# The third layer of an MLP on one Trainium2 core: its inputs as the fixed operand, the weight column moving, one answer a partition

## What is computed

```python
h = jnp.concatenate([z, dense_ctx], axis=1)      # 2048 x 208
h = jnp.maximum(h @ W_top1 + b_top1, 0.0)        # 208 -> 512
h = jnp.maximum(h @ W_top2 + b_top2, 0.0)        # 512 -> 256
y = h @ W_top3                                   # 256 -> 1, no bias
```

## Time and profile before

| what | value |
|---|---|
| median of three runs | 1182.02 us (1181.14 to 1182.32) |
| the profiled execution, its time | 1184.45 us |
| its span, first to last instruction | 1182.6 us |
| TensorE clock granted, mean | 0.99 of full speed |
| PE / PE weight load busy | 1118.4 us (95%) / 395.6 us (33%) |
| DVE / ACT / POOL busy | 1111.5 us (94%) / 835.7 us (71%) / 917.6 us (78%) |
| DMA packets, bytes | 76480, 167.32 MB |

### The profile page before, as it was taken

The page is one execution under the profiler, slowest core; times in us unless marked ns, Lnnn a source line. Parts: engine busy times, 40 slices in busy tenths (PEclk is TensorE's granted clock), DMA queues, the critical chain, the costliest instruction groups (busy, mean ns, idle before and its releaser), DMA issues.

```text
span 1182.6 us, 15683 instructions
## 1 busy us (share of the span) xinstructions
PE 1118.4 (95%) x5312; PEld 395.6 (33%) x5312; DVE 1111.5 (94%) x509; ACT 835.7 (71%) x2385; POOL 917.6 (78%) x640
## 2 busy tenths in 40 slices
PE   0587999999999999999999999999999999999997
PEld 0122233333333333333333333333333333333343
DVE  0598999999999999999999999999999999999994
ACT  0466577677868777686877778687767868777782
POOL 6767888888888888888888888888888888884400
PEclk9898999999999999999999999999999999999998
DMA  4895788767768876666887666788766668876200
GB/s 110 227 185 116 154 166 173 151 135 146 146 130 164 173 160 143 134 140 135 161 173 158 139 135 137 142 161 173 155 141 137 141 136 161 174 152 146 47 1 1
DMA packets 76480, 167.32 MB, mean 141 GB/s; under 512 B 22032, under 2 KB 39328, under 8 KB 76400
## 3 DMA queue, kind: packets, MB, share of 16 engines
q1 hardware_dynamic: 58704, 159.59, 64.0%
q0 software_dynamic: 16384, 4.23, 3.6%
q10 hardware_dynamic: 1312, 2.50, 0.8%
HBM read 157.86 MB, written 8.40 MB: 141 GB/s over the span
## 4 chain that ended last, share of the span: by engine, by line
PE 83%; DMA 6%; POOL 5%; issue 2%; ACT 1%; SPq 1%; ACTq 1%; DVE 0%; POOLq 0%; DVEq 0%
PE acc L643 77%; DMA q_tile<-x_of_steps 4%; POOL x_rows L260 4%; PE acc L716 3%; POOL p_l L272 2%; DMA x_rows<-in_table,ids_s 1%; PE acc L702 1%; PE acc L704 1%; DMA x_of_steps<-x_rows 1%; PE acc L724 1%; SPq L197 1%; ACTq L477 0%; SPq L225 0%; ACT xb L324 0%; ACT h L448 0%
## 5 line engine op out<-in xcount | busy, mean ns | idle before, releaser
L643 PE MATMUL acc<-p_dve,w_s 128*64 128x512 f32 x3840 | 855.9, 595 | 15.7 <-DVE p_dve L557 14.8
L260 POOL DMA_INDIRECT x_rows<-in_table,ids_s x512 | 491.8, 961 | 147.2 <-issue 130.9
L557 DVE TENSOR_TENSOR p_dve<-spread,xb 128x3072 f32<-128x3072 f32 (+2 forms) x224 | 566.1, 2585 | 4.7 <-issue 3.3
L557 DVE TENSOR_TENSOR p_dve<-spread,xa 128x2048 f32<-128x2048 f32 (+1 forms) x192 | 495.6, 2636 | 13.7 <-ACT xa L315 5.7
L643 PEld LDWEIGHTS acc<-p_dve,w_s 128*64 128x64 f32 x3840 | 271.2, 137 | 552.5 <-issue 486.8
L324 ACT ACTIVATE xb<-acc 32x512 f32<-32x512 f32 x512 | 288.8, 564 | 22.2 <-DVE p_dve L557 15.6
L272 POOL TENSOR_TENSOR p_l<-spread,q_tile 128x2048 f32<-128x2048 f32 x60 | 273.0, 4574 | 16.1 <-DMA q_tile<-x_of_steps 14.2
L315 ACT ACTIVATE xa<-acc 64x512 f32<-64x512 f32 x256 | 145.9, 570 | 152.7 <-PE acc L643 123.5
L283 POOL TENSOR_TENSOR p_pool<-spread,x_s 128x1024 f32<-128x1024 f32 x64 | 152.6, 2385 | 78.6 <-PE acc L643 37.3
L643 PE MATMUL acc<-p_l,w_s 128*64 128x512 f32 (+1 forms) x640 | 153.2, 613 | 38.5 <-ACT p_l L342 36.3
L333 ACT ACTIVATE x_s<-acc 64x512 f32<-64x512 f32 x256 | 151.6, 592 | 10.7 <-ACT y_row L467 4.8
(11 more groups left out here) (20 smaller groups left out, 202.9 us busy)
## 6 DMA issues: line engine op xcount, KB each, us to landing
spread<-x_of_steps SPq DMA_DIRECT2D x246, 512.0 KB, 17.5
q_tile<-x_of_steps SPq DMA_DIRECT2D x126, 128.0 KB, 11.4
x_rows<-in_table,ids_s POOLq DMA_INDIRECT x512
x_of_steps<-x_rows SPq DMA_DIRECT2D x64, 128.0 KB
spread<-x_of_steps SPq DMA_DIRECT2D x24, 128.0 KB, 4.3
w_s<-in_w SPq DMA_DIRECT2D x2, 512.0 KB, 6.4
spread<-x_of_steps ACTq DMA_DIRECT2D x8, 128.0 KB, 5.6
spread<-x_of_steps ACTq DMA_DIRECT2D x2, 512.0 KB, 12.2
```

The source lines that it names most:

```text
L260: nc.gpsimd.indirect_dma_start(out=x_rows[:, s % 2, i * DIM:(i + 1) * DIM], out_offset=None, in_=table, in_offset=bass.IndirectOffsetOnAxi ...
L557: nc.vector.tensor_tensor(p_dve[:, to:to + n, :], spread[:, s % 3, tile:tile + n, :], over(x[:], n), ALU.mult).then_inc(dve_made, n)
L643: last = nc.tensor.matmul(acc[b * K:(b + 1) * K, :], w, prod[:, b * BLK:(b + 1) * BLK], start=start, stop=stop)
```

## The change

The operands of the two matmuls change places: 128 columns of `h2` become the fixed operand and the one weight column moves. The answers come out as one column over 128 partitions, `acc0[:, 0:1]`. ACT copies this column into a tile of 128 partitions by one element, and the store writes 128 elements of four bytes from 128 partitions, where it wrote one run of 512 bytes from one partition. No wait and no place in any engine's order changes.

```diff
-        y_row = sb("y_row", [1, P])
+        y_col = sb("y_col", [P, 1])
...
-                nc.scalar.activation(y_row[:], acc0[0:1, 0:P], ACT.Copy).then_inc(mlp_done, 1)
+                nc.scalar.activation(y_col[:], acc0[:, 0:1], ACT.Copy).then_inc(mlp_done, 1)
                 act.wait_ge(mlp_done, 3 * t + 3)
-                act.dma_start(y[:, t * P:(t + 1) * P], y_row[:]).then_inc(y_stored, 16)
+                act.dma_start(y[:, t * P:(t + 1) * P].rearrange("o p -> p o"), y_col[:]).then_inc(y_stored, 16)
...
                 for k in range(H2 // P):
-                    last = nc.tensor.matmul(acc0[0:1, 0:P], wt3[:, k:k + 1], h2[:, k, :],
+                    last = nc.tensor.matmul(acc0[:, 0:1], h2[:, k, :], wt3[:, k:k + 1],
                                             start=(k == 0), stop=(k == H2 // P - 1))
```

## The result

The changed kernel takes 1204.22 us (median of four runs, 1199.94 to 1207.86) beside 1181.72 us for the kernel before: a ratio of 1.0176, interval 1.0159 to 1.0194. The prediction was 1182.4 us, 1180.6 to 1185.6. It missed by 22 us, nearly all from one line of the change, the store.

The account below looks back on a forecast made before the run. PE was taken to bound the kernel, with DVE nearly level. Terms of 0.0 on PE, 0.0 on ACT and queues, and 0.0 - 0.09 + 0.5 in the tail gave +0.4 on 1182.02: 1182.4 us, range 1180.6 to 1185.6.

Parts of the forecast that it names:

- PE: `mlp3` in the stream: the loads take the place of the streams, 0.53 us a call as before, so 0.0 us.
- the upper bound: `mlp3` on PE: each load waits until the matmul before it leaves the array; three times 163 ns, 0.49 us more a call.
- the first rival: `mlp3` on PE: loads and short matmuls take turns, up to 0.49 us a call, 7.3 us; 1189.7 us with the tail; chance 0.10.
- both PE rivals: `mlp3` on PE: load and matmul in turn, slower, 1189.7 us, chance 0.10; or loads hidden, faster, 1177.9 us, chance 0.05.
- the faster one: `mlp3` on PE: loads hidden, 0.43 us off a call, capped by DVE's 0.32; 4.5 us less, 1177.9 us; chance 0.05.
- ACT's two terms: ACT in the stream: the copy takes 0.18 us, 0.09 less; the store's issue takes 0.18 more, 0.43.
- ACT's cover: ACT in the stream: 2.9 us to spare between copy and `layer0`, so cost nothing; 1.5 us if all cover were gone.
- a wait of PE for `mlp_done`: Ahead of `layer0` on PE: a sign that ACT's cover was not there; no size given.
- The stores in the stream: DMA queues: 2032 packets more on 76480, engines busy 0.73 of a turn, next wait 69 us later; cost nothing.
- The tail: Last tile: PE unchanged, ACT's copy 0.09 us less, store 0.18 to 1.25 us longer, taken at 0.5; +0.4 us.
- The third rival: Last store only: 128 four-byte writes into the same 512 bytes go one after another; with 3 us, 1185.0 us; chance 0.04.

## Why the prediction was wrong, by its steps

**PE: right.** It summed to 0.53 us a call, against 0.53 before. Around the fifteenth tile after the change (timeline of PEld and PE; before):

```profile
1172.46 0.52 PEld L725 LDWEIGHTS acc<-wt,h 128*128 128x128 f32 x4 [0.81 <-issue]
1173.00 0.20 PEld L643 LDWEIGHTS acc<-p_dve,w_s 128*64 128x64 f32 x4
```

1173.00 - 1172.46 = 0.54 us. The four loads cover 0.52 us and last 0.19 each, so they are 0.11 apart: the loads have taken the place of the streams. The matmuls of one column are not "almost nothing" in the trace: their records last 0.25 us each, where those of 128 columns lasted 0.272, so the 163 ns taken as fixed in the upper bound were too few. The sum did not use them, and the next load starts while such a record still runs. By the Trainium skill's page "TensorE: Matmul & The Clock Gate", in the part on packing small matmuls, a load overlaps a matmul only in other row groups. That would have made this the first rival, 0.13 us or more a call; the trace disagrees, with loads of all 128 rows 0.11 us apart. The same section also lets a load go ahead that goes to the background weight buffer, a case that the prediction left out and that would allow what the trace shows. The operands alone, at a ratio of 1.0000, settle both PE rivals, the faster one too.

**ACT's two terms: right in size.** The copy was put at 0.18 us and takes 0.171; the issue at 0.43 and takes 0.362.

**ACT's cover: failed.** "I cost ACT at nothing here" rested on 2.9 us between the copy and `layer0`. ACT's copy and issue together became 0.02 us longer, which is nothing, but the cover was a distance in a turn where `q_tile` came on time. With the loads late, ACT was late ahead of `mlp3`, and PE's weight loads waited 15.0 us for the copy in nine turns, its matmuls 7.3 us in seven. I had named the sign, a wait of PE for `mlp_done`.

**The stores in the stream: failed, and this is the step of the 14.7 us.** I had the packets right (2032 more of data; 2272 in all, 78752 - 76480) and wrote "Cost: nothing", for two reasons: the engines were busy only 0.73 of the time, and the next wait for a store came a turn later. Both ask who waits for this store. Neither asks what it does to the transfers beside it. What the runs showed instead: the store alone makes the whole loss, the last gather of an odd step lands 2.4 us later in the mean, and PE's turn goes from 69.06 to 70.11 us. Nor had I read the gather loop, which was 1.85 us a turn from taking the bound over; the views I read showed PE and DVE level and stopped there. A fall of the clock behind a wait of PE was in no term either; at most 5.1 us go with it, by the estimate above.

**The tail: the term was mis-sized.** The store was bounded between 0.18 and 1.25 us and taken at 0.5; it is 6.2. The upper bound came from a load of 128 four-byte elements, landed in 2.0 us. A load of small elements from DRAM does not bound a store of small elements to one place there.

**The third rival** came nearest: writes into the same 512 bytes of DRAM that are slow at the end, with a chance of 0.04 and a price of 3 us. That they go one after another is not shown; half of them land in about the same time. Its size was half, and its place was wrong: "the last store only". The fifteen others cost more than twice as much, through others' transfers.

## What to carry to other kernels

Do not store a column of four-byte answers from 128 partitions into one contiguous run of DRAM: here such a store takes 7 us to land, and slows the DMA traffic beside it. Either keep the answers in one partition's row, or let them lie 64 bytes apart, which cost 0.4 us at the end and nothing in the stream. When a change alters only the shape of a transfer, price it twice, once for who waits for it and once for what is in flight beside it, and look for the loop through DRAM that has the least slack, not only for the busiest engine.

## What the runs showed of the hardware that was not expected

- 128 four-byte writes into 512 contiguous bytes land 7.0 to 8.4 us after the issue. All 144 packets of the last such store are through the engines by 1197 us, and the window from 1197 to 1203.5 us has no packet at all:

```profile
DMA packets 0, 0.00 MB, mean 0 GB/s; under 512 B 0, under 2 KB 0, under 8 KB 0
```

So in the tail the engines' records are over and the completion is late.
- While such a store is under way, gathers that have nothing to do with its address hold the engines five to eleven times as long (25.1 to 50.5% of the engines' time over 13 stores, against 3.1 to 5.7%, for about as many packets).
- The cost goes with how closely the elements lie: 7.3, 3.3, 2.4 and 1.5 us at 4, 8, 16 and 64 bytes, the issue taken off. Halving the number of elements leaves it at 6.9.
- In the steady part of the profiled execution the granted clock fell to 0.50 twice, for 6.8 and 3.4 us, each time behind a wait of PE for a copy, of 2.07 and 1.95 us.
